# Edge masks and layer 0 ahead of the next chunk's packing for chunks 0 to 25 of a two-layer graph kernel

## The reference

```python
# layer 0: adj holds no 2 or 3, so two of the three products vanish
o = (adj == 1) @ (x @ w1) + (adj == 2) @ (x @ w2) + (adj == 3) @ (x @ w3) + bias
x1 = layernorm(x + o)
# layer 1: attention over the edges
h = x1 @ W.T + b
e = (h @ we1 + be1) + (h @ we2 + be2).T
e = where(e >= 0, e, 0.01 * e)
out = layernorm(x1 + softmax(where(adj > 0, e, -9e15), axis=1) @ h)
```

## Time and profile before

| | us |
|---|---|
| median of 3 runs | 1519.58 (1518.77 to 1521.66) |
| the profiled execution: its own time | 1518.26 |
| the profiled execution: span of the core | 1516.3 |
| PE busy | 1410.2 (93%) |
| DVE busy | 1108.7 (73%) |
| ACT busy | 983.5 (65%) |

### The profile page before, as it was taken

The page is one execution under the profiler, slowest core; times in us unless marked ns, Lnnn a source line. Parts: engine busy times, 40 slices in busy tenths (PEclk is TensorE's granted clock), DMA queues, the critical chain, the costliest instruction groups (busy, mean ns, idle before and its releaser), DMA issues.

```text
span 1516.3 us, 19558 instructions
## 1 busy us (share of the span) xinstructions
PE 1410.2 (93%) x6934; PEld 668.3 (44%) x6934; DVE 1108.7 (73%) x2561; ACT 983.5 (65%) x1584; POOL 102.3 (7%) x137
## 2 busy tenths in 40 slices
PE   0877797999999999999999999999999999999996
PEld 0434353444444454444444444444444444444443
DVE  2667777987977967968869856777676777777563
ACT  1433526366457466556646648987888898898873
POOL 2111011110110101100111000000000000000000
PEclk9989899999999999999999999999999999999998
DMA  9999999995979779895798712000000010110000
GB/s 129 143 126 117 126 111 137 124 120 86 87 103 123 76 80 99 111 97 64 108 102 85 109 58 82 22 28 21 29 35 29 30 47 28 37 48 22 22 1 15
DMA packets 88980, 114.32 MB, mean 75 GB/s; under 512 B 5104, under 2 KB 71216, under 8 KB 88880
## 3 DMA queue, kind: packets, MB, share of 16 engines
q0 software_dynamic: 67584, 67.12, 48.3%
q1 hardware_dynamic: 21296, 45.92, 8.9%
HBM read 298.06 MB, written 16.29 MB: 207 GB/s over the span
## 4 chain that ended last, share of the span: by engine, by line
PE 66%; DVE 15%; DMA 10%; ACT 6%; issue 3%; POOL 0%; ACTq 0%; DVEq 0%; SPq 0%; POOLq 0%
PE ps L1258 50%; PE ps L1211 12%; DMA tables<-adj 8%; ACT neg_masks L1041 3%; DVE edge_masks L601 2%; DVE neg_masks L617 2%; DVE seen L582 1%; DMA e_scratch<-e_turned 1%; DMA e_row<-e_scratch 1%; PE ps L1220 1%; PE ps L1272 1%; DVE tables L689 1%; DVE a_c_rows L711 1%; DVE adj_in L579 1%; DVE h_part L677 1%
## 5 line engine op out<-in xcount | busy, mean ns | idle before, releaser
L1258 PE MATMUL ps<-pos_masks,tables 128*128 128x512 fp8e4 x2048 | 612.3, 381 | 17.2 <-DVE pos_masks L619 17.1
L1041 ACT ACTIVATE neg_masks<-e_row,cols 128x512 int8<-128x512 f32 x816 | 510.2, 709 | 61.3 <-PE ps L1258 54.7
L1258 PE MATMUL ps<-neg_masks,tables 128*128 128x512 fp8e4 x1632 | 488.4, 381 | 0.0
L1211 PE MATMUL ps<-edge_masks,tables 128*128 128x512 fp8e4 (+1 forms) x2048 | 461.9, 384 | 0.0
L1258 PEld LDWEIGHTS ps<-pos_masks,tables 128*128 128x128 f16 x2048 | 200.2, 98 | 259.7 <-issue 26.7
L1211 PEld LDWEIGHTS ps<-edge_masks,tables 128*128 128x128 f16 x2048 | 200.9, 99 | 231.9 <-issue 11.1
L1258 PEld LDWEIGHTS ps<-neg_masks,tables 128*128 128x128 f16 x1632 | 160.4, 98 | 194.8 <-issue 4.0
L601 DVE TENSOR_SCALAR pos_masks<-edges 128x512 uint16<-128x512 uint16 x512 | 114.5, 286 | 143.7 <-PE ps L1258 143.7
L1020 ACT ACTIVATE packed_bf<-packed 128x1024 bf16<-128x1024 uint8 x64 | 72.5, 1132 | 156.6 <-DVE packed L591 156.6
L617 DVE TENSOR_TENSOR neg_masks<-pos_masks,neg_masks 128x2048 uint16<-128x2048 uint16 x102 | 125.0, 1225 | 57.0 <-ACT neg_masks L1041 53.9
L1029 ACT ACTIVATE edges<-ps 128x1024 uint8<-128x1024 bf16 x64 | 65.0, 1016 | 154.8 <-PE ps L1220 154.8
(11 more groups left out here) (134 smaller groups left out, 864.9 us busy)
## 6 DMA issues: line engine op xcount, KB each, us to landing
adj_in<-adj POOLq DMA_DIRECT2D x84, 512.0 KB, 13.6
tables<-adj POOLq DMA_DIRECT2D x28, 512.0 KB, 32.5
e_row<-e_scratch SPq DMA_DIRECT2D x34, 256.0 KB, 4.1
edges<-adj POOLq DMA_DIRECT2D x16, 512.0 KB, 12.5
part_scratch<-a_c_rows SPq DMA_DIRECT2D x18, 256.0 KB, 4.9
part_in<-part_scratch SPq DMA_DIRECT2D x18, 256.0 KB, 4.0
edges<-x SPq DMA_DIRECT2D x8, 512.0 KB, 6.7
x_rows<-x SPq DMA_DIRECT2D x8, 512.0 KB, 6.5
```

Of the source, the lines that this page charges most:

```text
L1041: ins = e.activation(gate_bufs[GATE[m]][:, n:n + GR].bitcast(I8), e1row[:, q % 2, :], ACT.Sign, bias=t2[:, JC * c + j:JC * c + j + 1])
L1211: ins = e.matmul(ps[:, h, :], v_hl[:, i, JC * c + j, :], U0[:, n:n + GR].bitcast(kind), start=c == 0 and j == 0 and i == 0, stop=c == NCH ...
L1258: ins = e.matmul(z_bank(q, k), tab[:, c, 2 * k + i, j, :], mask[:, n:n + GR].bitcast(F8A), start=first and j == 0 and i == 0, stop=final a ...
```

## The change

For chunks below `SOON` = 26 the halves of `edge_masks` stand in DVE's slot ahead of the slot's masks and of `check_and_pack`, no longer behind it, and `layer0(c)` stands on PE in slot c+1 instead of c+2, so ahead of `turn(c+1)`. From chunk 26 on the order is the old one; slot 27 has no `layer0`. The tails of stripes 0, 1 and 2 (8 (S+1) at most 26) start a slot earlier, with `v_of`, `statistics` and `e_sums` ahead of the packing, and their batches are a slot nearer: batches 0 and 1 in slots 12 and 13, batches 2 to 7 in slots 20 to 26, batches 8 to 15 in slots 28 to 35. All other batches keep their slots; slot 36 has none.

```diff
--- before.py
+++ after.py
@@ -54,6 +54,15 @@
 
 START = 5
 
+SOON = 26
+
+
+def soon(S):
+
+    return int(NCH * (S + 1) <= SOON)
+
+
+
 EARLY = {
     0: [(0, [0]), (1, [0])],
     1: [(2, [0, 1]), (0, [1]), (1, [1]), (3, [0, 1])],
@@ -75,7 +84,7 @@
     for b, part in EARLY.items():
         segs += part
         n = sum(len(c) for _, c in part)
-        slots += [NCH * (b + 1) + START + (i * NCH // n if n >= 6 else i) for i in range(n)]
+        slots += [NCH * (b + 1) + START - soon(b) + (i * NCH // n if n >= 6 else i) for i in range(n)]
         for g, c in part:
             seen.setdefault(g, set()).update(c)
     for g in LATE:
@@ -122,7 +131,8 @@
 
 def fresh(m):
 
-    return SLOTS[m] == NCH * (BATCH[m][1] // 2 + 1) + START
+    S = BATCH[m][1] // 2
+    return SLOTS[m] == NCH * (S + 1) + START - soon(S)
 
 
 def first_of_all(m):
@@ -347,7 +357,11 @@
 
         def tails(k):
 
-            return [(S, k - 8 * (S + 1)) for S in range(NS) if 0 <= k - 8 * (S + 1) < 11]
+            return [(S, k + soon(S) - 8 * (S + 1)) for S in range(NS) if 0 <= k + soon(S) - 8 * (S + 1) < 11]
+
+        def layer0_at(k):
+
+            return [c for c in range(K) if k == c + (1 if c < SOON else 2)]
 
 
         G, NC2 = N // GR, N // GR
@@ -836,31 +850,40 @@
                 for S, off in tails(k):
                     if off == 2 and S < NS - 1:
                         v_of(S, 0)
+                if 1 <= k <= NCH:
+                    split_rest(k - 1)
+                if 1 <= k <= SOON:
+                    edge_masks(k - 1, 0)
+                    edge_masks(k - 1, 1)
                 for m in at(k):
                     if not first_of_all(m):
                         masks(m)
                         after(m)
-                if 1 <= k <= NCH:
-                    split_rest(k - 1)
+                for S, off in tails(k):
+                    if soon(S) and off == 2:
+                        v_of(S, 1)
+                        statistics(S)
+                    if soon(S) and off == 3:
+                        e_sums(S)
                 if k < K:
                     check_and_pack(k)
                 for S, off in tails(k):
-                    if off == 2:
+                    if off == 2 and not soon(S):
                         if S == NS - 1:
                             v_of(S, 0)
                         v_of(S, 1)
-                if 1 <= k <= K:
+                if SOON < k <= K:
                     edge_masks(k - 1, 0)
                 for S, off in tails(k):
-                    if off == 2:
+                    if off == 2 and not soon(S):
                         statistics(S)
-                    if off == 3 and S < NS - 1:
+                    if off == 3 and not soon(S) and S < NS - 1:
                         e_sums(S)
                     if off == 3 and S == NS - 1:
                         rs_of(S)
                     if off in (4, 6) and S == NS - 1:
                         e_sums(S, ((off - 4) // 2,))
-                if 1 <= k <= K:
+                if SOON < k <= K:
                     edge_masks(k - 1, 1)
                 for m in at(k):
                     if first_of_all(m):
@@ -1299,13 +1322,13 @@
 
             e.wait_ge(s_ident, 4)
             for k in range(NSLOT):
-                if 2 <= k < K + 2:
-                    layer0(k - 2, 0)
+                for c in layer0_at(k):
+                    layer0(c, 0)
                 for S, off in tails(k):
                     if off == 2 and S < NS - 1:
                         o_of(S, 1)
-                if 2 <= k < K + 2:
-                    layer0(k - 2, 1)
+                for c in layer0_at(k):
+                    layer0(c, 1)
                 for m in at(k):
                     if not first_of_all(m):
                         batch(m)
```

## The result

The changed kernel takes 1578.38 us (median of 6 runs, 1573.91 to 1584.67) against 1520.16 for the kernel before (1518.52 to 1521.66): ratio 1.0387, 95% interval 1.0362 to 1.0412. It is slower by some 58 us. The profiled execution, the fastest of the six, took 1573.91 us with a span of 1572.0, so its trace has to account for 55.7 us more span than before (1516.3).

The account below looks back on a forecast made before the run. PE bounds the kernel, with loads pacing slots 1 to 11. Terms 1.9 + 50.5 (29.9 + 32.2 - 11.6) + 8 = 60.4 on 1518.26 give 1578.7, stated as 1578 us; own range 1562 to 1594, with rivals 1548 to 1602.

Parts of the forecast that it names:

- The loads hide slots 1 to 8: Slots 1 to 8: 9.65 us fits into the loads' 10 to 11, cost nil; turning 8 at 117.5.
- Stripe 0's tail: Slots 9 and 10 take 16.4 and 16.3 us; turning behind batch 1 at 201.3 instead of 199.42, first term +1.9.
- The hand-over of 2.3 us: Slots 14 to 26: PE idles between turning and layer 0 while ACT and DVE work, thirteen times 2.3, +29.9 us.
- The tails' extras: Slots 17, 18, 20, 21, 26 and 27, where DVE or ACT is later than PE: sum 32.2 us.
- near 407: Time forecast for turning 27, at 354.74 before.
- The clock, +8: PE's matmuls partly run at 1.2 GHz behind idles: +8 us, with ends 0 and 16.
- Half of them: Of nine slots where PE rules with such an idle, half lose 1.6 us to the clock, giving 7 us.
- The slots 28 to 36 are as before but for the batch; slot 36 is short. I take nil.: Behind turning 27: no cost; the same pace as before.
- the 5 that was set as a sign of being wrong: Prediction is wrong if the time after turning 27 differs by more than 5 us from before.
- (a): Only the bubble: early tails cost nothing extra, slots overlap better; 30 us more, 1548 us; chance 0.12.
- (b): Clock falls in most slots, granted 0.85 over 200 us; its term is 30 instead of 8, 1600 us; chance 0.10.
- Rival (c): Faster: loads pace everything to chunk 27, so slot lengths don't count and batches lie nearer; 1509 us; chance 0.04.

Follow-up runs that it names:

- Run 3: Changed kernel, in slots 13 to 26 the slot's batch ahead of layer 0 on PE and its masks ahead of the edge masks on DVE; 1578.85 us, ratio 1.0393.
- run 2: Changed kernel with the three early tails' second addition, statistics and row sums behind the slot's packing instead of ahead of it; 1563.53 us, ratio 1.0292.
- run 4: Changed kernel with the gates of batches 0 and 2 behind the edges on ACT in slots 12 and 20; 1568.18 us, ratio 1.0323.
- run 5: Changed kernel with the new order for chunks 0 to 11 only, stripe 0's tail alone a slot nearer; 1521.65 us, ratio 1.0021.
- run 6: Changed kernel with the new order for chunks 0 to 19 only, tails of stripes 0 and 1 a slot nearer; 1553.13 us, ratio 1.0224.
- run 7: Changed kernel with the new order for chunks 0 to 7 only, stripe 0's tail alone a slot nearer; 1520.75 us, ratio 1.0013.
- run 10: Changed kernel, new order for chunks 0 to 11 only, with both repairs: statistics and row sums behind the packing, first gates behind the edges; 1513.03 us, ratio 0.9954.
- run 11: Changed kernel, new order for chunks 0 to 7 only, stripe 0's tail with statistics and row sums behind the packing; 1515.83 us, ratio 0.9978.
- run 8: Changed kernel with eight extra unused matmuls on PE behind turnings 14 to 18, in the idle ahead of layer 0; 1578.27 us, ratio 1.0390.
- run 9: Changed kernel, 26 chunks, statistics and row sums of the early tails behind the packing and first gates behind the edges; 1559.31 us, ratio 1.0263.

## Why the prediction was right

The way it went was forecast rightly, the slot lengths nearly so. That 1578 forecast and 1578.38 measured agree to 0.4 us is luck: the terms up to turning 27 were 12.5 us too high and the one behind it 7.8 too low, which leaves nearly 5 too much for the profiled execution (1578.7 against 1573.91), and this execution lies 4.5 below the median.

- *The loads hide slots 1 to 8.* Turning 8 is at 117.45; 117.5 was forecast.
- *Stripe 0's tail.* Slots 9 and 10 took 16.40 and 15.64 us, forecast 16.4 and 16.3. The end of batch 1 came at 199.15 instead of 201.3: the term +1.9 is -0.3. Batch 0 started at 178.43, forecast 178.6, and layer 0 of chunk 12 followed it without an idle, as batch 0 covered its hand-over.
- *The hand-over of 2.3 us.* From turning to layer 0 it is 2.66 us, forecast 2.75, and a plain slot is 9.57, forecast 9.65. Run 3 shows it going away beside a batch in slot 22.
- *The tails' extras.* Slot 17 took 16.40 (16.4), slot 18 15.64 (16.3), slot 20 27.63 (26.3), slot 21 16.48 (17.8), slot 26 20.09 (22.3), slot 27 4.71 (4.6). Runs 2 and 4 show two of the mechanisms, DVE ahead of the packing in slots 9, 10, 17 and 18, and ACT ahead of the edges in slots 12 and 20. In slot 26 the mechanism was another: not DVE's row set it but PE's own, an idle of 4.30 us behind x1 and the edges on ACT, a slow layer 0 and the batch. Slots 24 and 25 took 18.17 and 18.35 where the prediction has 16.6; in 25 it left out the two projections. Together turning 13 to 27 took 203.5 us; the forecast was 155.3 + 50.5 = 205.8, and 8 for the clock. Turning 27 came at 402.67; the "near 407" of the prediction leaves out its own 8 for the clock.
- *The clock, +8.* Between batch 1 and turning 27 PE was busy for 9.0 us more with the same work, but that is not 9.0 us of time: in slot 18 the slow layer 0 lies beside what DVE and ACT do. Slots 15, 20 and 24 show it in their length with 1.5 to 1.7 us each and slot 26 with some 1.2, as its packed bits were converted at 396.82 and turning 26 came at 397.96: 6 in all, and another 2.5 in slot 37. "Half of them" was too many: in this trace 2 of the 7 layers 0 that are whole and stand behind an idle of 2.05 us were slow.
- *"The slots 28 to 36 are as before but for the batch; slot 36 is short. I take nil."* This step was wrong. The slots to turning 36 do cost nothing (+0.5), but slot 36 without its batch takes the cover from stripe 3's first gates, and slot 37 costs 8.4 us, 5.9 of waiting and 2.5 of slow matmuls. The time after turning 27 differs by 7.8 us (8.4 + 0.5 - 1.2, rounded), more than the 5 that was set as a sign of being wrong. It made up for most of what the terms before it had too much: 2.2 at batch 1 and 10.3 (213.8 against 203.5) up to turning 27.

Of the rivals, (a) fails by the tails' slots, which were as long as drawn, and (b) by the grant of 0.92 over 203.5 us where it had 0.85. Rival (c), "faster", needed the loads to pace the chunks to 27. In the changed kernel the last wait of DVE for a load up to 330 us is ahead of the packing at 100.87, before stripe 0's tail. Runs 5 to 7, 10 and 11 fit its condition: a loss of more than 3 us only where the new order reaches into slots that PE paces. It is not shown what each of the thirteen idles costs alone; run 8 touched five, and the six executions of the change alone differ by 10.8 us.

## What to carry to other kernels

A consumer placed a step behind its producer pays for the whole hand-over around the engines once per step, unless something else stands between them on the engine that sets the pace; where another resource paces the loop, the same placement is nearly free (slots 1 to 8 took 90.2 us instead of 88.7) and can make later work start sooner. So ask of each stretch which resource paces it, and switch the order where that changes: of 8, 12, 20 and 26 chunks, 12 with both repairs was the fastest. A slot that loses its work also loses its cover: look at which round trip it hid.

## What the runs showed of the hardware

The runs of the changed kernel spread over 10.8 us where those of before spread over 3.1, and the granted clock goes with them: 0.974 in the run of 1573.91 us, 0.967 in that of 1584.67. The difference of 0.007 over some 1577 us is 11 us, an estimate that comes out at the spread itself. The spread of before is not always as small: in the 19 executions beside runs 5 to 8 it was 6.4 us (1516.76 to 1523.14).

An idle of the same length, 2.05 us, was followed by a layer 0 of 7.08 us in slot 14 and of 8.77 in slot 15 (the row at 211.38 above) of the same execution:

```profile
201.81 7.08 PE L1234 MATMUL ps<-edge_masks,tables 128*128 128x512 fp8e4 x32 [2.05 <-DVE edge_masks L615]
```

In the traces of the eight kernels with 20 or 26 chunks in the new order, 41 whole layers 0 stand behind an idle of just this length. 33 of them took 7.08 us, 8 took 8.72 to 8.77, and not in the same slots: slot 15 in the change, slot 16 in runs 2 and 4, none of slots 14 to 16 in runs 3, 6 and 9. Behind the idle of 3.9 to 4.3 us in slot 18 all six without a fill were slow. So a kernel with a short idle in every slot has its time partly decided by which of them are followed by slow matmuls; that this alone makes the spread is likely and not shown.
